# The end of an attention stage and the start of an expert stage: later weight splits, a shorter choice of two experts, and output biases moved to the last expert

## The reference

```python
# cross attention: 32 heads of 128 in 8 groups; rmsnorm on q and k
scores = einsum('bhqd,bhkd->bhqk', q, k) * scale + mask
out = softmax(scores) @ v          # then out @ o_proj_w.T
...
# mixture of 16 experts, 512 -> 128 -> 512, in 4 groups of 4
scores = softmax(xt @ router_w + router_b) + router_bias
keep   = the 2 groups with the largest maximum        # others masked to -inf
idx    = the 2 best experts among those kept          # lower index wins a tie
gate   = scores at idx, 0 elsewhere
y = sum_e gate[e] * ((silu(xt @ w1 + b1) * (xt @ w2 + b2)) @ w3 + b3)
z = silu(xt @ sw1 + sb1) * (xt @ sw2 + sb2) @ sw3 + sb3   # shared, inner width 256
```

## Time and profile before

| what | us |
|---|---|
| median of 3 runs | 880.07 (878.45 to 882.62) |
| the profiled execution | 883.29 |
| span of its profile | 881.5 |
| PE busy | 740.5 (84%) |
| DVE busy | 675.4 (77%) |
| ACT / POOL busy | 495.5 / 498.9 |

### The profile page before, as it was taken

One profiled execution on the slowest core, in us unless ns is written; L12 is line 12 of the kernel. 1 busy time (PEld: TensorE's weight loads), 2 busy tenths in 40 slices (PEclk: granted clock), 3 DMA queues, 4 the chain that ended last, 5 costly groups with the idle time before them and its releaser, 6 DMA issues.

```text
span 881.5 us, 14614 instructions
## 1 busy us (share of the span) xinstructions
PE 740.5 (84%) x3483; PEld 349.1 (40%) x3483; DVE 675.4 (77%) x1395; ACT 495.5 (56%) x900; POOL 498.9 (57%) x473
## 2 busy tenths in 40 slices
PE   0379879788780685799999999999999778999997
PEld 0134444343340233344444444444444233344443
DVE  6877768698999723788888888888888847466666
ACT  3333546566973301777777777777777524455551
POOL 2853636654767000678888888888884413244431
PEclk9869979799996696899999999999999978999999
DMA  7210013121102012467766666666645411223321
GB/s 312 72 60 0 1 48 119 48 72 48 49 1 95 0 39 91 79 165 176 184 146 147 145 149 146 146 146 148 144 95 96 96 37 36 95 87 105 107 71 48
DMA packets 147601, 84.84 MB, mean 96 GB/s; under 512 B 137185, under 2 KB 137441, under 8 KB 144626
## 3 DMA queue, kind: packets, MB, share of 16 engines
q1 hardware_dynamic: 147570, 84.47, 37.1%
HBM read 49.85 MB, written 1.05 MB: 58 GB/s over the span
## 4 chain that ended last, share of the span: by engine, by line
PE 63%; DVE 19%; issue 5%; ACT 4%; POOL 3%; DMA 2%; DVEq 1%; SPq 1%; ACTq 1%; POOLq 0%
PE ps L895 20%; PE ps L896 19%; PE ps L897 19%; DVE arena L1228 4%; ACT arena L598 3%; DVE arena L1225 3%; DVE arena L1222 2%; POOL arena L556 1%; PE ps L1089 1%; DVE dsc L1225 1%; DVE mm L1463 1%; DMA arena<-arena 1%; DVE arena L1491 1%; PE ps L962 1%; DVE arena L1560 1%
## 5 line engine op out<-in xcount | busy, mean ns | idle before, releaser
L895 PE MATMUL ps<-arena 128*128 128x512 f16 (+1 forms) x988 | 385.1, 390 | 30.7 <-DVE arena L1228 11.8
L896 PE MATMUL ps<-arena 128*128 128x512 f16 (+1 forms) x988 | 383.9, 389 | 0.0
L897 PE MATMUL ps<-arena 128*128 128x512 f16 (+1 forms) x988 | 383.2, 388 | 0.0
L598 ACT ACTIVATE arena<-arena 128x512 f32 (+7 forms) x372 | 248.1, 692 | 143.3 <-DVE arena L1228 33.3
L895 PEld LDWEIGHTS ps<-arena 128*128 128x128 f16 (+1 forms) x988 | 98.5, 100 | 151.7 <-issue 26.2
L1228 DVE SCALAR_TENSOR_TENSOR arena<-ps,arena 128x512 f32<-128x512 f32 (+2 forms) x182 | 123.2, 703 | 39.5 <-ACT arena L598 32.2
L897 PEld LDWEIGHTS ps<-arena 128*128 128x128 f16 (+1 forms) x988 | 98.8, 100 | 123.3 <-issue 11.8
L896 PEld LDWEIGHTS ps<-arena 128*128 128x128 f16 (+1 forms) x988 | 98.7, 100 | 111.0 <-issue 9.0
L556 POOL TENSOR_SCALAR arena<-arena,rden 128x512 f32<-128x512 f32 x128 | 114.0, 890 | 25.6 <-DVE rden L1580 16.5
L1222 DVE TENSOR_TENSOR arena<-arena 128x512 f16<-128x512 f32 (+3 forms) x143 | 115.1, 841 | 5.8 <-ACT arena L598 5.4
L598 ACT ACTIVATE arena<-ps 128x512 f16<-128x512 f32 (+4 forms) x114 | 64.2, 588 | 72.0 <-PE ps L936 36.8
(11 more groups left out here) (122 smaller groups left out, 732.8 us busy)
## 6 DMA issues: line engine op xcount, KB each, us to landing
arena<-in_moe_w SPq DMA_DIRECT2D x18, 768.0 KB, 4.4
arena<-in_ffn_w SPq DMA_DIRECT2D x33, 256.0 KB, 2.7
arena<-in_wq SPq DMA_DIRECT2D x8, 1024.0 KB, 5.0
arena<-in_wo SPq DMA_DIRECT2D x8, 1024.0 KB, 5.2
arena<-in_kv_w SPq DMA_DIRECT2D x4, 1024.0 KB, 5.0
arena<-in_ctx SPq DMA_DIRECT2D x1, 2048.0 KB, 9.4
arena<-in_ctx_t SPq DMA_DIRECT2D x1, 2048.0 KB, 13.8
arena<-arena SPq DMA_TRANSPOSE x128, 3.3
```

The lines of the kernel that those rows point to most:

```text
L598: return a.activation(out_, in_, ACT.Copy, scale=scale, bias=bias)
L895: pe.matmul(out_, lhs[0], rhs[0], start=first, stop=False)
L896: pe.matmul(out_, lhs[0], rhs[1], start=False, stop=False)
L897: return pe.matmul(out_, lhs[1], rhs[0], start=False, stop=last)
```

## The change

Five things are done:

1. The splits of experts 0 and 1 (`scale`, `high_in`, `high_out`, `low_in`, `low_out`) are moved behind the last probabilities: on ACT behind p_high(31), on POOL behind the scaling of step 31.
2. PE's order after values(31): the transposes of token tiles 0 to 2 come ahead of project(31); then hidden(0) for the first 384 token columns, the transposes of tile 3, the router, and hidden(0) for the last 128 columns (48 matmuls instead of 24, with the same columns in all). On DVE `expert_norm` of tiles 0 to 2 comes ahead of o_low(31), and the low parts of those tiles ahead of add_out(31).
3. The two best experts are found by maxima: `best` (a maximum, an equality, a product with a descending order, a maximum, an equality) is run, the winner is masked out, and `best` is run again; 14 instructions of at most 128 x 64 elements up to the gates. The first two products of expert 0 on DVE come ahead of the group choice.
4. The second half of the shared expert becomes the last of the 18 (`expert_at`), so a routed expert is second.
5. The bias matmuls are taken from expert 1 and put ahead of the products of the last expert, all four in front; the transposes of the gates move behind `experts_out(2)`.

```diff
@@ gpsimd
-            attention_step(HK - 1, 1, False)
-            attention_step(HK - 1, 2, False)
+            for s in range(1, 4):
+                attention_step(HK - 1, s, False)
             low_in(0, 0)
-            attention_step(HK - 1, 3, False)
+            rstd(3, 0, NT - 1)
             low_out(0, 0)
-            rstd(3, 0, NT - 1)
             low_in(1, 1)
@@ scalar
-            scale(0)
-            attention_step(HK - 1, 1, False)
-            scale(1)
-            q_square(last)
-            exponentials(last - 1)
-            q_high(last)
-            a.wait_ge(a_q, HK * NT)
-            high_in(0, 0)
...
+            for s in range(1, 3):
+                attention_step(HK - 1, s, False)
...
                 p_high(last, h)
+            scale(0)
+            high_in(0, 0)
+            high_out(0, 0)
+            scale(1)
             high_in(1, 1)
             o_high(last)
...
-            expert_step(0, 0)
-            expert_step(0, 1)
+            for e in range(3):
+                expert_step(e // 2, e % 2)
             gates_out()
@@ tensor
+            def experts_out(e, q):
+                biases = isinstance(e, int) and e == EX - 1
+                if biases:
+                    for t in range(NT):
+                        pe.wait_ge(m_x, (e - 1) * NT + t + 1)
+                        pe.matmul(bank(4 + t), gt[0:NE + 1, 0, t * P:(t + 1) * P], b3[0:NE + 1, 0], start=True,
+                                  stop=False)
+                pe.wait_ge(m_hl, e + 1)
...
             project(HK - 1, 2)
             values(HK - 1, 3)
+            for t in range(NT - 1):
+                expert_transposes(t)
             project(HK - 1, 3)
-            for t in range(NT):
-                expert_transposes(t)
-
+            pe.wait_ge(xe_lo, NT - 1)
+            hidden(0, 0, ((0, TOK - P),))
+            expert_transposes(NT - 1)
...
-            hidden(0, 0)
+            hidden(0, 0, ((TOK - P, TOK),))
             hidden(1, 1)
             experts_out(0, 0)
+            for e in range(1, 3):
+                hidden(e + 1, (e + 1) % 2)
+                experts_out(e, e % 2)
             pe.wait_ge(gates_ready, 1)
-            pe.wait_ge(m_v, 1)
+            pe.wait_ge(m_v, 3)
@@ vector
-            o_low(HK * NT - 1)
             for h in range(R):
                 v.wait_ge(a_tr[h], 16 * HK * NT)
             expert_norm(3, 0, 3)
+            o_low(HK * NT - 1)
+            for t in range(3):
+                expert_low(t)
             add_out(HK - 1, 3)
...
+            expert_hidden(0, 0)
...
-            ranks(rank, masked, NE)
-            own.link(ts(rank, rank, 2.0, ALU.is_lt))
+            def best(src, dst):
+
+                own.link(v.tensor_reduce(top, src, AX.X, ALU.max))
+                own.link(tt(dst, src, over(top, NE), ALU.is_equal))
+                own.link(tt(dst, dst, order.unsqueeze(1).broadcast_to([P, NT, NE]), ALU.mult))
+                own.link(v.tensor_reduce(top, dst, AX.X, ALU.max))
+                own.link(tt(dst, dst, over(top, NE), ALU.is_equal))
+
+            best(masked, rank)
+            own.link(stt(masked, rank, -4.0e30, masked, ALU.mult, ALU.add))
+            best(masked, second)
+            own.link(tt(rank, rank, second, ALU.add))
```

More of the change, by code:

```diff
@@ L826, in high_out @@
                 copy(me[0][:, q, 2 * D:3 * D], one(me_raw, e % ER)[:, 2 * D:3 * D]).then_inc(m_hi_out, 1)
[L828 to L832, removed]
-            last = HK * NT - 1
-            scale(0)
-            attention_step(HK - 1, 1, False)
-            scale(1)
-            q_square(last)
-            exponentials(last - 1)
-            q_high(last)
-            a.wait_ge(a_q, HK * NT)
-            high_in(0, 0)
+            last = HK * NT - 1
+            for s in range(1, 3):
+                attention_step(HK - 1, s, False)
             for h in range(R):
[L844 to L847, removed]
+                a.wait_ge(a_sm, 4 * last + h + 1)
+                a.activation(sc[:, h], sc[:, h], ACT.Exp, bias=mneg[:, h:h + 1], scale=-1.0,
+                             accum_out=den[:, h:h + 1]).then_inc(a_e, 1)
             for h in range(R):
@@ L1152, in expert_transposes, with hidden @@
                 mm.then_inc(xe_ps, 1)
+            def hidden(e, q, pieces=((0, TOK),)):
+                pe.wait_ge(m_lo_in, e + 1)
+                if not isinstance(e, int) or e >= 2:
+                    pe.wait_ge(m_v, e - 1)
+                for lo, hi in pieces:
+                    for i in range(2):
+                        if not isinstance(e, int) and i == 1:
+                            pe.wait_ge(g_c, 1)
+                        for k in range(KD):
+                            lhs = [w[:, q, i * D + k * P:i * D + (k + 1) * P] for w in me]
+                            mm = product(bank(2 * q + i)[:, lo:hi], lhs, [h[:, k, lo:hi] for h in xt], k == 0, k == KD - 1)
+                        if hi == TOK:
+                            mm.then_inc(m_h, 1)
+            def experts_out(e, q):
[6 more added lines that the diff above has]
+                pe.wait_ge(m_hl, e + 1)
+                pe.wait_ge(m_lo_out, e + 1)
+                for t in range(NT):
+                    if biases:
+                        pass
+                    elif not isinstance(e, int) or e >= 1:
+                        pe.wait_ge(m_x, (e - 1) * NT + t + 1)
+                    elif t == NT - 1:
+                        pe.wait_ge(r_sub, 1)
+                    product(bank(4 + t), [h[:, q, t * P:(t + 1) * P] for h in ht],
+                            [w[:, q, 2 * D:3 * D] for w in me], not biases, True).then_inc(m_y, 1)
             project(HK - 1, 2)
             values(HK - 1, 3)
+            for t in range(NT - 1):
+                expert_transposes(t)
             project(HK - 1, 3)
-            for t in range(NT):
-                expert_transposes(t)
+            pe.wait_ge(xe_lo, NT - 1)
+            hidden(0, 0, ((0, TOK - P),))
+            expert_transposes(NT - 1)
             pe.wait_ge(xe_lo, NT)
@@ L1168, in _ @@
             mm.then_inc(r_ps, 1)
[L1170 to L1188, removed]
-                    elif t == NT - 1:
-                        pe.wait_ge(r_sub, 1)
-                    biases = isinstance(e, int) and e == 1
-                    mm = product(bank(4 + t), [h[:, q, t * P:(t + 1) * P] for h in ht],
-                                 [w[:, q, 2 * D:3 * D] for w in me], True, not biases)
-                    if biases:
-                        mm = pe.matmul(bank(4 + t), gt[0:NE + 1, 0, t * P:(t + 1) * P], b3[0:NE + 1, 0], start=False,
-                                       stop=True)
-                    mm.then_inc(m_y, 1)
-            hidden(0, 0)
+            hidden(0, 0, ((TOK - P, TOK),))
             hidden(1, 1)
             experts_out(0, 0)
+            for e in range(1, 3):
+                hidden(e + 1, (e + 1) % 2)
+                experts_out(e, e % 2)
             pe.wait_ge(gates_ready, 1)
-            pe.wait_ge(m_v, 1)
+            pe.wait_ge(m_v, 3)
             for t in range(NT):
@@ L1206, in _ @@
             mm.then_inc(g_t, 1)
-            for e in range(1, 3):
-                hidden(e + 1, (e + 1) % 2)
-                experts_out(e, e % 2)
             with pe.Fori(1, EX // 2 - 1) as j:
```

53 lines of the change are left out of this document (34 added, 19 removed).

## The result

The changed kernel takes 870.13 us in the median (869.32 to 872.54, 4 runs) beside 881.35 us for the kernel before; the ratio is 0.988, with a 95% interval of 0.9844 to 0.9917. It is 11.2 us shorter, where 16.1 were forecast (864.0 from a median of 880.07), and its time lies just above the range, which ended at 869.5. The profiled execution has a span of 867.5 us against 881.5.

What follows compares the result with a forecast made beforehand. PE was taken as the bound: busy at full clock except in the rearranged stretches, where it stops and runs slow. Terms -2.8 - 0.2 - 9.9 - 6.4 + 3.2 = -16.1 us took 880.07 to 864.0; range 860.5 to 869.5.

Steps and rivals of the forecast that it cites:

- A: End of attention, up to the end of values(31): 2.8 us less, bounds 0 and 4.4 less.
- B: From the end of values(31) to the end of the router: 12.0 us against 12.25, so 0.2 less.
- D: From hidden(2) to the end of hidden(17): bias matmuls and the slow clock behind the gates leave, 6.4 us less.
- T: The time at which the router ends, 722.19 us in the kernel before.
- C: From the router's end to the start of hidden(2): 20.2 us before, 9.9 less forecast.
- E: The end, behind hidden(17): nothing hides the four biases, 3.2 us more (3.1 to 3.4).
- Rival 1: The clock falls in the new order too, around hidden(0) and hidden(1): gain 11.3 to 15 us, 868 taken; chance 0.15.
- Rival 4: The choice of two experts becomes a wait, plus late weights: 2 to 4 us back, 866 to 868; chance 0.05.
- Rivals 2, 3 and 5: End of attention holds its time, 867 (0.08); more gained, 860.7 (0.09); slower, clock stays 1.2 GHz, 885 or more (0.03).

Runs made afterwards that it cites:

- splits as before: Changed kernel with the splits of experts 0 and 1 back where they stood on ACT and POOL in the kernel before: 874.67 us, ratio 0.9927.

## Why the prediction was right or wrong

The direction held, and so did A with B, and D, to 0.4 us. The step that failed is "From T to hidden(2) (C)", where the text says that ten small instructions take 2.4 us, "and the low part, 0.7": they took 4.2 and 1.5, because POOL's subtractions for experts 1 and 2 ran against them. E was too small as well. The stages fall 3.6 us short of the forecast (12.5 for 16.1); C is 2.7 of it and E 1.0.

The median is 6.1 us above the forecast of 864.0. Besides the 3.6 us, 1.3 come from the median before, which is now 881.35 and was 880.07; the rest, 1.2, no profile assigns. The range was left by only 0.6, so that any one of three shares alone, C's, E's or that of the median before, takes the time out of it; C's is the largest.

- *A and B*, -3.0 forecast, -3.4 measured. The low parts of step 30 are faster with POOL's subtraction gone (3.1 us in all, as said), the transfer becomes the next bound (a stop of 1.60), and ACT's five pieces fit (the row below). Putting the splits back brought the slow row and the stop back. ACT's timeline in the changed kernel, two high parts and the five pieces, in 6.59 us from 695.09; o_high(31) follows at 705.41:

```profile
695.09 6.59 ACT L609 ACTIVATE arena<-arena 128x512 f16<-128x512 f32 x7
```

- *C*, -9.9 forecast. Out(0) starts 10.4 us behind T instead of 7.7, so C measured about -7.2. The small products waited out low_in(2), and the low part ran against low_out(1): 1.8 and 0.85 us. With these two subtractions made small out(0) started at T + 7.7 and the middle stage gave -16.0, against -16.3 forecast for C and D. (The terms up to T + 4.7 add up to 4.5; the trace has 4.7.) The prediction had read this very effect in the earlier trace rows, and had even placed it on the normalisation (where it appeared: 4.00 us for three instructions, hidden but for about 0.2, an estimate), but did not ask what POOL would be doing under the group choice.
- *D*, -6.4 forecast, about -6.1 measured: the bias pairs and the fall behind the gates are gone.
- *E*, +3.2 forecast (bounds 3.1 to 3.4), +4.2 measured. The order of waits was right, the pairs cheaper (3.70 for four, not 4.2 to 4.5), and the products behind them ran at 0.62 of the clock. That the clock would fall there was not considered. The fall is 1.6 of it; at full clock E is 2.6 (12.99 against 10.37).
- *Rival 1* (the clock) was not the whole story but a real part: both profiles of the changed kernel have one fall between router and hidden(2), and where it comes decided 2.4 us; in the first of them it cost this stage nothing. The gain of its median was 11.2 us in the first comparison and 7.5 in the second, which fits, though the times alone do not show it.
- *Rival 4* (the choice as a wait) had the right engine, but neither the place nor the cause: the 14 instructions stand behind expert 0's low part and took 3.6 us, as forecast. The wait came ahead of out(0), in the group choice, by POOL's interference. *Rivals 2, 3 and 5* did not come.
- The choice by maxima was credited with 6 us of DVE time. It is 3.3; the rest of what ranks cost before was the same interference. In the one execution with ranks put back it brought nothing.

- The reading of the clock, a fall to 1.2 GHz behind each stop of 2.60 us and more, does not hold beyond the kernel before: behind 2.81 us (splits as before) and 2.75 (changed) it stayed at 2.4. The length of the stop alone does not decide.
- "Up to 688.8 us it is busy in every microsecond" is shown from 657 us on, where the earlier trace rows begin. PE's 740.5 us in a span of 881.5 leave 141 idle, about 22 of them behind 657.

The Trainium skill's page "GPSIMD Engine Reference" gives the contention in its row on SBUF interfaces (with instructions of two SBUF inputs or in a two-port mode). The run with small subtractions agrees: 2.32 us to 0.50 for two such instructions, 1.54 to 0.69 for the third. In which mode the slowed normalising instructions ran, of one SBUF input each, no trace here shows.

What stays open: what decides in which stretch the clock falls from one execution to the next, and why the first 687 us, in which PE's work is the same in all, vary by almost 5.

## What to carry to other kernels

When a stage is moved or shortened on one engine, ask what the engine beside it will be doing in each new overlap, not only in the old one; here a subtraction on POOL turned a 0.25 us instruction into 2 us. Work that is needed late (gates) should not stand ahead of work that the bound engine needs next: moving it behind took away the stop of 2.75 us and, in four profiles of four, the clock's fall, and brought the middle stage to 16.0 us below before, where 16.3 were forecast. And an amount of work moved to the end of the kernel must be priced with what hides it there (nothing: 2.6 us here) and with the clock of what follows it (1.6 more).

## What the runs showed of the hardware

- DVE instructions with two SBUF inputs are held up by a POOL subtraction of two inputs, even small ones: one of 128 x 64 elements took 2.07 us (0.25 without it) under a subtraction of 2.13. It goes the other way too: in the kernel before the four wide comparisons took 2.8 us more (7.65 for 4.86), and the two subtractions beside them 2.66 and 2.14 us for 2.13 and 1.14. The additions that read PSUM and one SBUF tile were not slowed (four in 2.72 us, under low_in in the later experts). Three normalising instructions, of one SBUF input, took 4.00 us under two subtractions, and 1.45 in the kernel before.
- Four 17-row fp32 bias pairs in a row were followed, or overtaken, by a fall to 1.2 GHz in six of seven profiles; the same pairs between products of 128 rows in none of four.
